# Softmax denominators of an attention kernel: one 1024-column add per key block in place of two of 512, mostly on GpSimd, and eight probability buffers in place of six

## What is computed

```python
HEADS, HEAD_DIM = 16, 64
q = hidden_states @ Wq          # 2048 x 1024
k = encoder_hidden_states @ Wk  # 1601 x 1024
v = encoder_hidden_states @ Wv
logits = jnp.einsum('bhqd,bhkd->bhqk', q, k) * scale + col_bias
probs = jax.nn.softmax(logits, axis=-1)
out = jnp.einsum('bhqk,bhkd->bhqd', probs, v)
out = out @ Wo + bo + residual
```

## Time and profile before

| what | value |
|---|---|
| runs before, median of 3 | 5466.34 us (5460.77 to 5468.5) |
| span of the profiled execution | 5460.9 us |
| PE busy | 5173.7 us, 95% |
| PE weight load busy | 2708.9 us, 50% |
| DVE busy | 3684.8 us, 67% |
| ACT busy | 2245.5 us, 41% |
| POOL busy | 2695.0 us, 49%, in 2048 instructions |
| chain that ended last | PE 82%, issue 7%, DVE 6%, DMA 2% |
| mean granted PE clock | 0.969 |

### The profile page before, as it was taken

One profiled execution on the slowest core, in us unless ns is written; L12 is line 12 of the kernel. 1 busy time (PEld: TensorE's weight loads), 2 busy tenths in 40 slices (PEclk: granted clock), 3 DMA queues, 4 the chain that ended last, 5 costly groups with the idle time before them and its releaser, 6 DMA issues.

```text
span 5460.9 us, 81559 instructions
## 1 busy us (share of the span) xinstructions
PE 5173.7 (95%) x21484; PEld 2708.9 (50%) x21484; DVE 3684.8 (67%) x5908; ACT 2245.5 (41%) x4042; POOL 2695.0 (49%) x2048
## 2 busy tenths in 40 slices
PE   7999999999979898987999999999989999999999
PEld 4455545554444444444455555555445455545554
DVE  6767676767667676765767666676676667676767
ACT  2433344334425455552444444344424444444443
POOL 1656565656510101011656566666625656565655
PEclk8999999999979999997999999999989999999999
DMA  2010101010020101001010101010011010101010
GB/s 72 14 27 14 27 14 27 14 27 14 14 43 15 24 16 23 16 15 26 14 26 13 26 13 26 13 26 19 8 28 24 16 26 13 26 13 26 13 26 17
DMA packets 40356, 116.57 MB, mean 21 GB/s; under 512 B 7350, under 2 KB 20150, under 8 KB 35068
## 3 DMA queue, kind: packets, MB, share of 16 engines
q1 hardware_dynamic: 39938, 112.04, 9.4%
HBM read 26.86 MB, written 2.10 MB: 5 GB/s over the span
## 4 chain that ended last, share of the span: by engine, by line
PE 82%; issue 7%; DVE 6%; DMA 2%; SPq 1%; ACT 0%; DVEq 0%; POOL 0%; ACTq 0%; POOLq 0%
PE OB L654 19%; PE SS L594 13%; PE ST L625 11%; PE ST L627 9%; PE ST L551 5%; PE ST L567 4%; PE OB L786 4%; DVE mpart L1087 4%; PE ST L765 3%; PE SS L744 3%; PE ST L572 3%; PE ST L672 3%; PE ZB L607 2%; DMA Q<-rawQ 1%; PE ZB L744 1%
## 5 line engine op out<-in xcount | busy, mean ns | idle before, releaser
L282 POOL TENSOR_TENSOR acc<-acc,P 128x512 f32<-128x512 f32 (+1 forms) x1776 | 2362.5, 1356 | 455.1 <-ACT P L934 308.8
L934 ACT ACTIVATE P<-ST 128x512 f32<-128x512 f32 (+1 forms) x2496 | 1385.5, 597 | 2012.0 <-PE ST L627 1703.7
L1087 DVE TENSOR_REDUCE mpart<-SS 128x1 f32<-128x400 f32 (+1 forms) x3072 | 1665.0, 563 | 764.1 <-PE SS L594 709.1
L654 PE MATMUL OB<-P,V 128*64 128x512 f32 (+1 forms) x4992 | 1348.0, 618 | 1.1
L594 PE MATMUL SS<-KS,Q 128*128 128x400 f32 (+1 forms) x3072 | 1171.6, 387 | 70.2 <-DVE mpart L1087 67.1
L625 PE MATMUL ST<-Q,K 128*128 128x512 f32 (+1 forms) x2496 | 1061.3, 425 | 32.9 <-issue 18.3
L594 PEld LDWEIGHTS SS<-KS,Q 128*128 128x128 f32 x3072 | 585.0, 192 | 860.0 <-DVE mpart L1087 758.5
L627 PE MATMUL ST<-Q,K 128*128 128x512 f32 (+1 forms) x2496 | 989.6, 396 | 0.0
L278 POOL TENSOR_TENSOR acc<-P 128x512 f32<-128x512 f32 x192 | 241.3, 1278 | 1410.8 <-ACT P L934 1310.8
L625 PEld LDWEIGHTS ST<-Q,K 128*128 128x128 f32 (+1 forms) x2496 | 462.8, 185 | 515.8 <-ACT P L934 348.3
L1106 DVE RECIPROCAL R<-ZB 128x64 f32<-128x64 f32 (+1 forms) x432 | 371.3, 860 | 408.9 <-PE ZB L607 408.9
(11 more groups left out here) (126 smaller groups left out, 3608.1 us busy)
## 6 DMA issues: line engine op xcount, KB each, us to landing
Q<-Q SPq DMA_DIRECT2D x48, 512.0 KB, 4.5
KS<-K SPq DMA_DIRECT2D x48, 400.5 KB, 3.8
K<-K SPq DMA_DIRECT2D x48, 400.5 KB, 5.3
Q<-Q SPq DMA_DIRECT2D x32, 256.0 KB, 4.3
wk<-in_wk SPq DMA_DIRECT2D x25, 256.0 KB, 4.4
wv<-in_wv SPq DMA_DIRECT2D x25, 256.0 KB, 4.6
Q<-rawQ SPq DMA_DIRECT2D x16, 256.0 KB, 3.8
wq<-in_wq SPq DMA_DIRECT2D x25, 128.0 KB, 4.3
```

What stands on the lines that cost most here:

```text
L282: eng.tensor_tensor(out, out, P[0:rows_of(t), u % NP, :], ALU.add).then_inc(done, raised)
L654: last = pe.matmul(OB[64 * jj:64 * jj + 64, :], V[0:k, t, 64 * b:64 * b + 64], P[0:k, (2 * s + jj) % NP, :], start=t == 0, stop=t == KT - 1)
L934: act.activation(P[0:k, u % NP, :], ST[u % 4][0:k, :], ACT.Exp, scale=SCALE).then_inc(act_p, 1)
L1087: dve.tensor_reduce(mpart[:, i // len(KCH), i % len(KCH):i % len(KCH) + 1], SS[i % 2][:, 0:w], AX.X, ALU.max).then_inc(dve_s, 1)
```

## The change

It makes one add for each step over both chunks, 128 x 1024, where there were two of 128 x 512 (`add_step` for `add_unit`); it waits for the exponentials of both chunks and for the add of the step before. Ownership goes by step: DVE has the one at t = 6, POOL the other eleven of a half; in a last head DVE has t = 3, 6, 9 and 12. `P` has 8 buffers for 6, so that both chunks of a step lie side by side, and ACT reuses one eight units later; it waits for the add only at the first chunk of a step. `sums` has one wait for two. The middle layer and the loads name the first six buffers of `P`, as before.

```diff
-NP = 6
+NP = 8
...
     owner = {}
-    for u in range(UNITS):
-        t, jj = u // 2 % KT, u % 2
+    for step in range(STEPS):
+        t = step % KT
         if t > 0:
-            owner[u] = "dve" if jj == 1 and t >= 2 and (alone or t % 4 == 0) else "pool"
-    at = {u: UNITS if u == max(v for v in owner if owner[v] == e) else u + 1 for u, e in owner.items()}
+            owner[step] = "dve" if t == 6 or alone and t >= 2 and t % 3 == 0 else "pool"
+    at = {e: UNITS if e == max(v for v in owner if owner[v] == owner[e]) else 2 * e + 2 for e in owner}
     return owner, at
...
-        def add_unit(eng, name, pr, g, u, alone):
+        def add_step(eng, name, pr, g, s, alone):
 
             owner, at = adds(alone)
-            if owner.get(u) != name:
+            if owner.get(s) != name:
                 return
-            t, out, done = u // 2 % KT, acc[0:rows_of(u // 2 % KT), u // (2 * KT), u % 2, :], acc_sem[name]
-            raised = at[u] - max([at[v] for v in owner if owner[v] == name and v < u], default=0)
-            pr.wait(act_p, 2 * UNITS, g * UNITS + u + 1)
+            c2, t, k, done = s // KT, s % KT, rows_of(s % KT), acc_sem[name]
+            raised = at[s] - max([at[v] for v in owner if owner[v] == name and v < s], default=0)
+            now, before = (P[:, 2 * i % NP:2 * i % NP + 2, :] for i in (s, s - 1))
+            pr.wait(act_p, 2 * UNITS, g * UNITS + 2 * s + 2)
             if t == 1:
                 pr.wait(pe_z, 4, 2 * g)
-                eng.tensor_tensor(out, P[:, (u - 2) % NP, :], P[:, u % NP, :], ALU.add).then_inc(done, raised)
+                eng.tensor_tensor(acc[:, c2, :, :], before, now, ALU.add).then_inc(done, raised)
             else:
 
-                pr.wait(acc_sem[owner[u - 2]], 2 * UNITS, g * UNITS + at[u - 2])
-                eng.tensor_tensor(out, out, P[0:rows_of(t), u % NP, :], ALU.add).then_inc(done, raised)
+                pr.wait(acc_sem[owner[s - 1]], 2 * UNITS, g * UNITS + at[s - 1])
+                out = acc[0:k, c2, :, :]
+                eng.tensor_tensor(out, out, now[0:k], ALU.add).then_inc(done, raised)
...
-                for jj in range(2):
-                    wait_added(pr, g, (c2 + 1) * 2 * KT - 2 + jj, alone)
+                wait_added(pr, g, (c2 + 1) * KT - 1, alone)
...
                             pr.wait(pe_pv, 2 * STEPS, g * STEPS + v // 2 + 1)
-                            wait_added(pr, g, v, alone)
+                            if v % 2 == 0:
+                                wait_added(pr, g, v // 2, alone)
...
-                    for u in (2 * s, 2 * s + 1):
-                        add_unit(dve, "dve", pr, g, u, other is None)
+                    add_step(dve, "dve", pr, g, s, other is None)
```

More of the change, by code:

```diff
@@ L179, in attention_layers @@
         gwo = rawK[:, (2 * CCT + CT) * 128:(2 * CCT + CT) * 128 + C]
-        K4hi = P[:, :, :].rearrange("p n q -> p (n q)")[:, 0:KP].bitcast(F32R)
+        K4hi = P[:, 0:6, :].rearrange("p n q -> p (n q)")[:, 0:KP].bitcast(F32R)
         K4lo = acc[:, :, :, :].rearrange("p a b q -> p (a b q)")[:, 0:KP].bitcast(F32R)
         Q4hi, Q4lo = Q2[0], rawQ[:, :].bitcast(F32R)
-        PG = [P[:, i, :] for i in range(NP)] + [acc[:, i // 2, i % 2, :] for i in range(3)]
+        PG = [P[:, i, :] for i in range(6)] + [acc[:, i // 2, i % 2, :] for i in range(3)]
         Z = acc[:, 1, 1, :]
@@ L266, in attention_layers, with wait_added @@
         gpool_on = sem("gpool_on")
-        def add_unit(eng, name, pr, g, u, alone):
+        def add_step(eng, name, pr, g, s, alone):
             owner, at = adds(alone)
-            if owner.get(u) != name:
+            if owner.get(s) != name:
                 return
-            t, out, done = u // 2 % KT, acc[0:rows_of(u // 2 % KT), u // (2 * KT), u % 2, :], acc_sem[name]
-            raised = at[u] - max([at[v] for v in owner if owner[v] == name and v < u], default=0)
-            pr.wait(act_p, 2 * UNITS, g * UNITS + u + 1)
+            c2, t, k, done = s // KT, s % KT, rows_of(s % KT), acc_sem[name]
+            raised = at[s] - max([at[v] for v in owner if owner[v] == name and v < s], default=0)
+            now, before = (P[:, 2 * i % NP:2 * i % NP + 2, :] for i in (s, s - 1))
+            pr.wait(act_p, 2 * UNITS, g * UNITS + 2 * s + 2)
             if t == 1:
                 pr.wait(pe_z, 4, 2 * g)
-                eng.tensor_tensor(out, P[:, (u - 2) % NP, :], P[:, u % NP, :], ALU.add).then_inc(done, raised)
+                eng.tensor_tensor(acc[:, c2, :, :], before, now, ALU.add).then_inc(done, raised)
             else:
-                pr.wait(acc_sem[owner[u - 2]], 2 * UNITS, g * UNITS + at[u - 2])
-                eng.tensor_tensor(out, out, P[0:rows_of(t), u % NP, :], ALU.add).then_inc(done, raised)
-        def wait_added(pr, g, u, alone):
+                pr.wait(acc_sem[owner[s - 1]], 2 * UNITS, g * UNITS + at[s - 1])
+                out = acc[0:k, c2, :, :]
+                eng.tensor_tensor(out, out, now[0:k], ALU.add).then_inc(done, raised)
+        def wait_added(pr, g, s, alone):
             owner, at = adds(alone)
-            u = u + 2 if u // 2 % KT == 0 else u
-            pr.wait(acc_sem[owner[u]], 2 * UNITS, g * UNITS + at[u])
+            s = s + 1 if s % KT == 0 else s
+            pr.wait(acc_sem[owner[s]], 2 * UNITS, g * UNITS + at[s])
         block = ctx.enter_context(nc.Block())
@@ L304, in _ @@
                              .rearrange("(t p) c -> p t c", p=128)).then_inc(d_x, 16)
[L305 removed]
+            sp.dma_start(P[:, 0:6, :], a["ctx"][0:768, :].rearrange("(t p) c -> p t c", p=128)).then_inc(d_in, 16)
             sp.dma_start(acc[:, :, :, :].rearrange("p a b c -> p (a b) c"),
@@ L477, in pair @@
                 for g in range(2):
-                    for u in range(UNITS):
-                        add_unit(gp, "pool", pr, g, u, last and g == 1)
+                    for s in range(STEPS):
+                        add_step(gp, "pool", pr, g, s, last and g == 1)
             def big_layer(l):
```

## The result

The changed kernel takes 5550.58 us (median of 4 runs, 5549.11 to 5553.99) against 5463.89 us (4 runs, 5460.77 to 5468.5) for the kernel before: 1.0157 times as long, with a 95% interval of 1.0144 to 1.0170. That is 87 us more. The profiled execution took 5551.44, of which 5549.6 are its span, 88.7 more than the span of before. The mean granted clock of TensorE is 0.969 in it, as before.

What follows compares the result with a forecast made beforehand. PE, busy 95%, bounds the kernel, so adds cost only where PE waits. Even heads +48, odd heads +25, ends of heads +12 and last heads +2 make +87 us on the 5466.3 median: 5553, range 5450 to 5620.

Steps and rivals of the forecast that it cites:

- The exclusion: DVE and POOL take turns by whole instructions; a 1024-column POOL add of 2.35 us holds DVE out for 2.21.
- (a): Even heads, step 4: `lo_part` meets POOL's fourth add and waits 1.45 us, so PE stalls 1.0.
- (b): Even heads: DVE's own 1024-column add of 1.24 us at step 6 delays the next maximum; PE stalls 0.75.
- (d): Even heads: DVE's add at step 19 with a 0.55 us reciprocal piece behind it stalls PE 0.6 at step 20.
- (c): Even heads, steps 8 to 11: DVE and POOL alternate in turns of 2.75 us, costing PE 0.5 in all.
- Odd heads: Two opening divisions wait for POOL, +1.1 us at step 2; with later stalls 3.3 against 2.1, +25 over 21 heads.
- Ends of even heads: The last division waits for POOL's last add, delaying `negm` and the transpose: +0.5 us in 24 heads, +12.
- Last heads: The sums wait for a serial chain of adds that ends some 0.7 us later, in three heads: +2.
- No new collisions: Rival, chance 0.12: `lo_part` falls into POOL's pause and old stalls go; 5433 us for half, 5400 for all.
- Collisions missed, long adds felt: Rival, chance 0.06: only the stalls from DVE's own two long adds stay; -8 us, 5458, no change.
- Slower instruction: Rival, chance 0.10: POOL's add takes 2.56 us and its step exceeds PE's; +151 us, 5617.
- Code loading: Rival, chance 0.06: shorter code shifts PE's 3 us stands at loop-backs; -18 us if gone, +36 if later layers get them.

Runs made afterwards that it cites:

- the first experiment: The changed kernel with each POOL add cut into two instructions of 512 columns, DVE's add left at 1024: 5498.7 us, ratio 1.0053.
- the four kernels with moved pieces: `lo_part` subtractions moved to other steps: kernel before 5399.59 us; changed kernel 5534.36, then placed again 5473.7; changed kernel with DVE's adds moved too 5407.53.

## Why the prediction was right, step by step

- **The exclusion.** Right, and the step that everything hangs on. A DVE operation that met POOL's add of 1024 columns was held until 2.25 after that add's start, by the row above; I took 2.21. The add takes 2.38 (I took 2.35; two of the old ones take 2.56). The Trainium skill's rule of an exclusive lock (SBUF — State Buffer, "two separate sides") agrees with all of these rows, but for the last 0.13 us of a POOL add, in which the DVE operation already ran. Cut to 512 columns, 52 us came back.
- **POOL's pace.** Two adds in a row stand 2.52 apart (2.38 and 0.14 between them); I took 2.51. The claim that POOL gains nothing in throughput holds: it is busy 2654 us for 2695.
- **(a), step 4 of even heads.** 1.27 for my 1.0. The mis-sized term is the start of POOL's first add: 0 + 1.07 for 0 + 0.9. The fourth exponential ends at 0 + 0.85 (3333.83 + 2.06 for the mark at 3335.04), and POOL begins 0.22 behind that; I allowed 0.05, although show about 0.26 from the third exponential (some 0.5 before 3294.69) to the old first add at 3294.43. The four adds shift by as much: 0.17 x 24 = 4 us. The rest, 0.1, is spread over terms too small to tell apart.
- **(b), step 7.** 0.88 for 0.75, and (d), step 20, 0.59 for 0.6. **(c), steps 8 to 11,** 0.51 for 0.5. The sum of the even head is 68.63 - 66.26 = 2.37 for my 2.0: 55 us for 48, the largest error in the sum: 0.27 a head from (a) and 0.13 from (b).
- **Odd heads.** Step 2 has 1.12 for 1.1: the two divisions, asked at 3428.47, 2.45 behind mark 0, end at 6.7 for the 6.6 that I worked out, and PE stands behind them:

```profile
3428.47 4.21 DVE L1121 TENSOR_TENSOR On<-Oraw,R 64x512 f32<-64x512 f32 x2
3432.61 1.68 DVE L1089 TENSOR_REDUCE mpart<-SS 128x1 f32<-128x402 f32 x3
...
3433.23 0.45 PE L596 MATMUL SS<-KS,Q 128*128 128x400 f32 x1 [0.84 <-DVE mpart L1089]
```

  The others are 0.45, 0.53, 0.24 + 0.38 + 0.12 and 0.47 for 0.5, 0.7, 0.5 and 0.5: 3.3 in total, as worked out. +24.2 us for +25. That (c) came out at 0.74 and (b) at 0.53 is two errors that cancel.
- **Ends of even heads.** The division behind the last step holds `negm` (3405.28, 2.24, then 3407.55; the earlier trace rows): +0.36 for +0.5, in 21 heads for 24 (the three behind which the last pair ends scatter too much to tell), so 7.6 us for 12.

```profile
3405.28 2.24 DVE L1121 TENSOR_TENSOR On<-Oraw,R 64x512 f32<-64x512 f32 x1
3407.55 0.22 DVE L1094 TENSOR_REDUCE negm<-mpart 128x16 f32<-128x64 f32 x1
...
3407.82 0.28 PE L601 MATMUL SS<-ident,negm 128*16 128x128 f32 x1 [0.18 <-DVE negm L1094]
```

- **Last heads.** The wait of the sums, 0.85 in the earlier trace rows, is 0.69, 0.85 and 0.85 in the three last heads before and 1.33, 1.41 and 1.41 after: 0.56 to 0.64 longer for my 0.7, 1.8 us for 2. In the distances between layers the scatter hides it.
- **Buffers.** Costed at nothing, measured at nothing (0.999). The reading behind it was wrong: the 304 us of the earlier trace rows are not waits for adds (see the run with eight buffers). That eight buffers are needed to cover POOL's lateness behind DVE's add isn't shown. In the changed kernel's trace the add that ACT needs had ended at least 2.8 us before; by the same working the one six units back, as six buffers would need it, had ended at least 0.5 before. No run has the long adds with six buffers.
- **The rivals.** "No new collisions" failed on its condition, the phase: `lo_part` met the add and not the pause. Its mechanism is real, though: where the phase was moved, the ceiling that it named came out (5407.53 and 5399.59, for the 5400 of "all of it"). "Collisions missed, long adds felt" fell too: (b) and (d) cost what it said, but (a) came on top. "Slower instruction" fell with the 2.38. "Code loading": the stand of some 3 us at layer 0's six loop-backs is in every kernel of the study and at no other layer's loop-backs (18.3 us in all before, 18.4 after), so it moved nothing.
- **The sum** is 87 measured for 87 by the medians, 88.7 by the spans, but the terms are off by +7 in even heads, -1 in odd ones and -4 at the ends: together 2 too few, as the spans say. That the sum is nearer than they are is luck.
- **What the profile should show.** The marks came within 0.3 of those given. Wrong was "medians above 1.2" for the two `lo_part` operations:

```profile
L1078 DVE TENSOR_TENSOR K<-rawK,K x192: 553/574/2411, 49.2 to 5410.8; 64x400 fp32r<-64x400 f32 x144, 64x402 fp32r<-64x402 f32 x48
...
L1081 DVE TENSOR_TENSOR Q<-rawQ,Q x192: 677/1161/1907, 56.6 to 5421.3; 64x512 fp32r<-64x512 f32 x192
```

  (minimum/median/longest in ns). A head has four `K<-rawK,K`. The first two are held (2.23 and 0.93 in the even head above), the last two take 0.57, since POOL is waiting for DVE's add at that time or has only just got it; the median of 574 lies among the free ones and hides the one in a head that costs 1.27. `Q<-rawQ,Q` has 1161, and a longest of 1907 for my "over 2.2".

What stays open: what the stand of DVE at a loop-back is (the last section has its size), and whether the long adds would do with six buffers.

## What to carry to other kernels

Where two engines take turns at something, ask of every merge how long one instruction of it is, and who asks at which moment; the same number of elements in half as many instructions saved 930 instructions here and cost 87 us. Before changing the work, try moving it: in a loop that repeats to a hundredth of a microsecond, eight small operations at other steps gave 68 us (1.3%), more than any form of the add. A place that is good by the mean can be the worst there is, so read the phase off the timeline of each kind of head, the ones right behind a loop-back too. And before a row of the list of waits is believed, look up when the instruction it names was needed and when it was done.

## What the runs showed of the hardware

- A POOL add of 128x1024 takes 2.38 us and one of 128x512 1.28, so twice the columns cost 1.86 times; on DVE it is 1.22 for 0.69, 1.77 times.
- An add of 1024 columns on POOL that needs the one before it starts 0.14 us behind it; the earlier trace rows has 0.20 for one of 512. A waiting DVE operation gets its turn at the end of the running one in the rows shown here, between two POOL adds that don't depend on each other as well (the rows of the first experiment), and then POOL's second add waits for it and takes 1.61 for 1.29.
- At the loop-back of a pair of heads in the last two layers DVE stands with nothing named, 2.43 us at 3307.18 above and 2.4 to 3.0 in all twelve of them in the four kernels with moved pieces, where PE doesn't stand. It matters only for what is first behind it.
- A stall of 4 us costs more than itself: steps 2 and 3 of the head below are 5.7 us longer than their usual time, with PE idle for 3.98. In this head, one of those with the blocked pieces (mark 0 at 3674.57), the clock granted to PE was 1.00 of full speed up to 3679.5. It was 0.87 in the mean over each of the stretches 3679.5 to 3686.5 and 3686.7 to 3692.0, so for a part of both it was at the lower of its two levels (1.2 for 2.4 GHz), and at 1.00 again from 3692. The four P·V matmuls behind the stall took 1.73 for 1.08:

```profile
3684.93 0.70 PE L597 MATMUL SS<-KS,Q 128*128 128x400 f32 x1 [3.98 <-DVE mpart L1090]
...
3686.74 1.73 PE L656 MATMUL OB<-P,V 128*64 128x512 f32 x4
```
